# Output rows of a chunked attention: seven block products of 256 columns per pair of chunks in place of eight

## The reference, cut to what matters

```python
o = jnp.transpose(_chunk_abc(q, k, v, s), (0, 2, 1, 3))      # 16 heads, 64 slots, values of 128
g = (hidden_states @ Wg).reshape(b, t, H, DV)
o = o * jax.lax.rsqrt(jnp.mean(jnp.square(o), axis=-1, keepdims=True) + EPS) * g_norm_weight
o = o * (g * jax.nn.sigmoid(g))
return o.reshape(b, t, VALUE_DIM) @ Wo                        # VALUE_DIM = 2048, Wo is 2048 x 512
...
x = _layernorm(x + _L0_attn_ref(x, ...), axis=-1)
```

## Time and profile before

| | |
|---|---|
| median of 3 runs | 1337.37 us (1337.26 to 1337.68) |
| the profiled execution, its own time | 1337.4 us |
| its span, first to last instruction | 1335.7 us |
| TensorE busy | 1326.4 us, 99% |
| VectorE busy | 813.2 us, 61% |
| ScalarE busy | 473.0 us, 35% |
| GpSimd busy | 276.4 us, 21% |
| mean granted TensorE clock | 0.999 |

### The profile page before, as it was taken

The page is one execution under the profiler, slowest core; times in us unless marked ns, Lnnn a source line. Parts: engine busy times, 40 slices in busy tenths (PEclk is TensorE's granted clock), DMA queues, the critical chain, the costliest instruction groups (busy, mean ns, idle before and its releaser), DMA issues.

```text
span 1335.7 us, 20339 instructions
## 1 busy us (share of the span) xinstructions
PE 1326.4 (99%) x8160; PEld 1143.3 (86%) x8160; DVE 813.2 (61%) x1559; ACT 473.0 (35%) x1391; POOL 276.4 (21%) x254
## 2 busy tenths in 40 slices
PE   9999999999999999999999999999999999999998
PEld 7888888888888888888888888888888888888886
DVE  5665666556666565656655566666556667656754
ACT  5333333343333433333234333343333333432221
POOL 3012311132112301231113111231023113122211
PEclk9999999999999999999999999999999999999999
DMA  6000200010000100010001000010000210000010
GB/s 205 17 1 0 56 1 16 1 32 25 16 1 25 32 17 1 9 48 5 12 0 48 10 17 1 25 32 17 1 22 27 64 33 0 1 0 32 18 46 32
DMA packets 35357, 31.73 MB, mean 24 GB/s; under 512 B 7617, under 2 KB 28097, under 8 KB 35265
## 3 DMA queue, kind: packets, MB, share of 16 engines
q1 hardware_dynamic: 35264, 30.44, 7.6%
HBM read 26.24 MB, written 4.19 MB: 23 GB/s over the span
## 4 chain that ended last, share of the span: by engine, by line
PE 97%; DVE 1%; DMA 0%; ACT 0%; issue 0%; POOLq 0%; SPq 0%; POOL 0%
PE p L899 20%; PE p L901 19%; PE p L900 19%; PE t L948 5%; PE s L973 3%; PE o L1090 3%; PE xb L1045 2%; PE o L1026 2%; PE o L1024 2%; PE t L1090 2%; PE p L973 2%; PE s L1379 2%; PE s L1381 2%; PE s L1380 2%; PE xb L998 2%; PE o L1023 2%
## 5 line engine op out<-in xcount | busy, mean ns | idle before, releaser
L899 PE MATMUL p<-wvg_hi,xt_hi 128*128 128x512 f32 x512 | 206.0, 402 | 0.1
L900 PE MATMUL p<-wvg_lo,xt_hi 128*128 128x512 f32 x512 | 199.8, 390 | 0.0
L901 PE MATMUL p<-wvg_hi,xt_lo 128*128 128x512 f32 x512 | 199.8, 390 | 0.0
L542 ACT ACTIVATE v_tok<-p 128x256 f32<-128x256 f32 x128 | 49.8, 389 | 318.8 <-PE p L901 318.8
L708 DVE SCALAR_TENSOR_TENSOR gate<-th,p 128x256 f32<-128x256 f32 x128 | 54.0, 422 | 164.4 <-ACT th L546 160.9
L899 PE MATMUL p<-xt_hi,wsqk_hi 128*128 128x512 f32 x380 | 148.4, 391 | 0.0
L900 PE MATMUL p<-xt_lo,wsqk_hi 128*128 128x512 f32 x380 | 148.2, 390 | 0.0
L901 PE MATMUL p<-xt_hi,wsqk_lo 128*128 128x512 f32 x380 | 147.8, 389 | 0.0
L491 POOL TENSOR_TENSOR orstd<-ovar,minus_half 128x8 f32<-128x8 f32 x32 | 52.4, 1639 | 447.1 <-DVE ovar L843 447.1
L482 POOL TENSOR_TENSOR v_lo<-v_tok,v_hi 128x256 fp32r<-128x256 f32 x96 | 83.8, 886 | 198.9 <-ACT v_hi L551 198.9
L901 PEld LDWEIGHTS p<-wvg_hi,xt_lo 128*128 128x128 f32 x512 | 96.1, 188 | 21.3
(11 more groups left out here) (241 smaller groups left out, 2844.0 us busy)
## 6 DMA issues: line engine op xcount, KB each, us to landing
raw<-in_L_attn_Wv SPq DMA_DIRECT2D x32, 128.0 KB, 2.4
raw<-in_L_attn_Wg SPq DMA_DIRECT2D x32, 128.0 KB, 2.9
raw<-in_L_attn_Wo SPq DMA_DIRECT2D x16, 256.0 KB, 2.8
out<-acc SPq DMA_DIRECT2D x16, 256.0 KB, 2.1
acc<-in_L_attn_hidden_states SPq DMA_DIRECT2D x3, 1024.0 KB, 7.5
raw<-in_L_attn_Ws SPq DMA_DIRECT2D x8, 256.0 KB, 2.8
raw<-in_L_attn_Wq SPq DMA_DIRECT2D x8, 256.0 KB, 2.8
raw<-in_L_attn_Wk SPq DMA_DIRECT2D x8, 256.0 KB, 3.3
```

The lines of the kernel that those rows point to most:

```text
L542: nc.scalar.activation(v_tok[:, c, :], PB[bk][:, 0:VW], ACT.Copy).then_inc(v_done, 1)
L899: nc.tensor.matmul(out_, lh, rh, start=(k == 0), stop=False)
L900: nc.tensor.matmul(out_, lh, rl, start=False, stop=False)
L901: last = nc.tensor.matmul(out_, ll, rh, start=False, stop=(k == n - 1))
```

## The change

The rows of two chunks a and b by the two heads are seen as a 2x2 matrix of blocks (A11 = chunk a, head 0; A12 = chunk a, head 1; A22 = chunk b, head 1; A21 = chunk b, head 0), and the weights as a 2x2 matrix of blocks of 128x256. Their product is formed from seven block products in place of eight (Winograd's form). Three of them use blocks of y (M1, and M2 with M4 in one bank), four use sums S1 to S4 of blocks of y; the weights get sums T1 to T4. A product is still three matmuls, now of 256 columns: 42 in a cell. The 2x2 of sums of results is formed by accumulating in PSUM (U2 onto M1's bank, C onto M5's bank, the last product onto U2's) and by VectorE, which adds each bank to `acc` at each of these states: eight additions of 256 columns and four of 512.

- VectorE: `y_sums`, four sums of 128x128 per half, the first half's ahead of `keep_keys(1)`; `y_low` of 384 columns.
- ScalarE: `y_high` copies A21 apart (128 columns) and the high part of three blocks; `sums_high`, the high part of S1 to S4; `rows_scaled`, `rows_high` for the weights.
- GpSimd: `sums_low` twice at the beginning of its part of a cell; `row_sums`, `row_lows` for the weights once per pair of heads.
- TensorE: new waits, for `s_lo_done` before M5, and before a bank is accumulated onto for VectorE's reading of it (`m1_read`, `m5_read`, `u2_read`).
- Buffers move, `wo` has seven blocks, TensorE's turn of pz waits for `c_read`, its weights products for `added`; in the last cell the turns of V wait for `added`.

```diff
-P_USES = ["vg0", "vg1", "wo0", "wo1", "wo2", "wo3", "vg2", "vg3", "s", "q", "k", "a0", "a1"]
+P_USES = ["vg0", "vg1", "wo0", "wo1", "vg2", "vg3", "s", "q", "k", "a0", "a1"]
...
+        def row_sums(pool, J):
+            w1, w2 = row_pieces
+            t = sums[:].rearrange("p h a t -> p (h a t)").rearrange("p (k n) -> p k n", k=4)
+            pool.wait_ge(wo_scaled, 2 * (J + 1))
+            nc.gpsimd.tensor_tensor(t[:, 0, :], w1[:, HALF:D], w1[:, 0:HALF], ALU.subtract).then_inc(wo_summed, 1)
...
+        def sums_low(pool, prev, i):
+            pool.wait_ge(s_hi_done, prev.count(2, i + 1))
+            nc.gpsimd.tensor_tensor(s_lo[i][:], sums[:, i, :, :], s_hi[i][:].bitcast(F32),
+                                    ALU.subtract).then_inc(s_lo_done, 1)
+
+        def cell_gpsimd(pool, cell, J=None, wo_J=None, last=False):
+            if not first(cell):
+                sums_low(pool, cell.shifted(-1), 0)
+                sums_low(pool, cell.shifted(-1), 1)
...
+            nc.scalar.activation(a21[:, half, :], Y_BANK[half][:, 3 * P:], ACT.Copy).then_inc(a21_done, 1)
+            nc.scalar.activation(yt_hi[:, half, :, :].rearrange("p a t -> p (a t)"), Y_BANK[half][:, 0:3 * P],
                                  ACT.Copy).then_inc(yt_hi_done, 1)
+
+        def sums_high(act, cell, half):
+            act.wait_ge(s_summed, cell.shifted(-1).count(8, 4 * half + 4))
+            nc.scalar.activation(s_hi[half][:], sums[:, half, :, :], ACT.Copy).then_inc(s_hi_done, 1)
...
             if not first(cell):
                 act.wait_ge(ok_summed, cell.count(1, 1))
                 slots_high(act)
                 values_high(act, cell, 0)
+                sums_high(act, cell, 1)
...
+        def y_sums(dve, cell, half):
+            prev = cell.shifted(-1)
+            blk = Y_BANK[half][:].rearrange("p (a t) -> p a t", a=CH)
+            out_ = sums[:, half, :, :]
+            dve.wait_ge(yt_hi_done, prev.count(2, half + 1))
+            nc.vector.tensor_tensor(out_[:, S1, :], a21[:, half, :], blk[:, A22, :], ALU.add).then_inc(s_summed, 1)
+            nc.vector.tensor_tensor(out_[:, S3, :], blk[:, A11, :], a21[:, half, :], ALU.subtract).then_inc(s_summed, 1)
+            dve.wait_ge(s_summed, prev.count(8, 4 * half + 1))
+            nc.vector.tensor_tensor(out_[:, S2, :], out_[:, S1, :], blk[:, A11, :], ALU.subtract).then_inc(s_summed, 1)
+            dve.wait_ge(s_summed, prev.count(8, 4 * half + 3))
+            nc.vector.tensor_tensor(out_[:, S4, :], blk[:, A12, :], out_[:, S2, :], ALU.subtract).then_inc(s_summed, 1)
...
             gate_vector(dve, cell, 0)
             keep_keys(0)
             gate_vector(dve, cell, 1)
+            if not first(cell):
+                y_sums(dve, cell, 0)
             keep_keys(1)
             keep_keys(2)
             if not first(cell):
                 y_low(dve, cell, 0)
+                y_sums(dve, cell, 1)
                 y_low(dve, cell, 1)
...
             if not first(cell):
-                add_rows(dve, cell, 1)
+                add_m1(dve, cell, 1)
+                add_m24(dve, cell, 1)
+                add_m5(dve, cell, 0)
+                add_m5(dve, cell, 1)
+                add_u2(dve, cell, 0)
+                add_u2(dve, cell, 1)
...
+            for i in range(2):
+                bk, before = p_turn(cell, f"wo{i}")
+                wait_read(pe, p_read, before)
+                pe.wait_ge(yt_lo_done, prev.count(2, i + 1))
+                row_product(SB[i][:, 0:HALF], parts[i], A11, B11, True, m1_done)
+                row_product(PB[bk][:, 0:HALF], parts[i], A12, B21, True, None)
+                row_product(PB[bk][:, HALF:D], parts[i], A22, T4, True, m24_done)
+            for i in range(2):
+                pe.wait_ge(s_lo_done, prev.count(2, i + 1))
+                row_product(C_BANK[i][:, 0:HALF], mixed[i], S1, T1, True, m5_done)
+            for i in range(2):
+                pe.wait_ge(m1_read, prev.count(2, i + 1))
+                row_product(SB[i][:, 0:HALF], mixed[i], S2, T2, False, u2_done)
+            for i in range(2):
+                pe.wait_ge(m5_read, prev.count(2, i + 1))
+                row_product(C_BANK[i][:, 0:HALF], mixed[i], S4, B22, False, c_done)
+            for i in range(2):
+                pe.wait_ge(u2_read, prev.count(2, i + 1))
+                row_product(SB[i][:, 0:HALF], mixed[i], S3, T3, False, a_done)
...
             if last:
+                pe.wait_ge(added, cell.count(2, 0))
                 car.prep_turn(pe, 0, PREP[0])
```

More of the change, by code:

```diff
@@ L604, in cell_scalar @@
             values_high(act, cell, 2)
+            if wo_J is not None and wo_J > 0:
+                rows_scaled(act, wo_J)
             act.wait_ge(pz_turned, cell.count(1, 1))
@@ L621, in cell_scalar @@
                 keys_scalar(act, nxt)
-            if wo_J is not None:
-                for i in (7, 8):
-                    split_high(act, wo_J, i, (rows, wo_J * (B * CH)))
             if last:
@@ L755, in cell_vector @@
+        def cell_vector(dve, cell, last=False):
             nxt = cell.shifted(1)
@@ L953, in turned_y @@
             pe.wait_ge(y_done, cell.count(2 * CH, 0))
-            turned(Y_BANK[half], [y[:, c, h, :] for c in (2 * half, 2 * half + 1) for h in range(2)], y_turned)
-        def output_rows(pe, cell, c):
-            prev = cell.shifted(-1)
-            bk, before = p_turn(cell, f"wo{c}")
-            wait_read(pe, p_read, before)
-            pe.wait_ge(yt_lo_done, prev.count(2, c // 2 + 1))
-            if c == 0:
-                if prev.batch == 0:
-                    pe.wait_ge(wo_lo_done, (prev.b // B) * 2 + 2)
-            split_product(PB[bk][:], [((yt_hi[:, c // 2, c % 2, h, :], yt_lo[:, c // 2, c % 2, h, :]),
-                                       (wo_hi[:, h, :], wo_lo[:, h, :])) for h in range(2)], rows)
+            a, b = 2 * half, 2 * half + 1
@@ new lines, in turned_y, with row_product @@
+            turned(Y_BANK[half], [y[:, a, 0, :], y[:, a, 1, :], y[:, b, 1, :], y[:, b, 0, :]], y_turned)
+        def row_product(out_, left, which, right, begin, done):
+            hi, lo = left
+            nc.tensor.matmul(out_, hi[:, which, :], wo_hi[:, right, :], start=begin, stop=True, skip_group_check=True)
+            nc.tensor.matmul(out_, hi[:, which, :], wo_lo[:, right, :], start=False, stop=True, skip_group_check=True)
+            mm = nc.tensor.matmul(out_, lo[:, which, :], wo_hi[:, right, :], start=False, stop=True, skip_group_check=True)
+            if done is not None:
+                mm.then_inc(done, 1)
@@ new lines, in output_rows @@
+        def output_rows(pe, cell):
+            prev = cell.shifted(-1)
+            if prev.batch == 0:
+                pe.wait_ge(wo_lo_done, (prev.b // B) * 4 + 4)
+            parts = [(yt_hi[:, i, :, :], yt_lo[:, i, :, :]) for i in range(2)]
+            mixed = [(s_hi[i], s_lo[i]) for i in range(2)]
+            for i in range(2):
[14 more added lines that the diff above has]
+                row_product(C_BANK[i][:, 0:HALF], mixed[i], S4, B22, False, c_done)
+            for i in range(2):
+                pe.wait_ge(u2_read, prev.count(2, i + 1))
+                row_product(SB[i][:, 0:HALF], mixed[i], S3, T3, False, a_done)
```

229 lines of the change are left out of this document (156 added, 73 removed).

## The result

The changed kernel takes **1463.86 us** (median of 4 runs, 1459.88 to 1468.61) against 1337.47: ratio 1.0946, 95% interval 1.0929 to 1.0963. That is 126.4 us more; the forecast was 99 more, and its range ended at 1455, 9 us short.

A forecast was written before the change was run, and what follows sets the result against it. TensorE, busy 99% of the span, was taken to bound the kernel. Cell stalls 84, weight-split cells 11, last cell 2.4 and tail 2 made 99 us on 1337.4: 1436 us, range 1392 to 1455.

The forecast's parts named there:

- Steps 1 to 6: One cell's queues put in order on its clock: stalls 3.25 less 0.6, +2.7 us per cell, 31 cells, +84 us.
- stall 2: TensorE's M5 of half 1 waits for GpSimd's low parts of the sums: 0.65 us.
- stall 3: TensorE's U2 of half 1 waits for VectorE's third addition, which reads the same bank: 1.1 us.
- stall 4: TensorE's product C waits for VectorE's first addition of M5, which reads the same bank: 0.7 us.
- stall 5: TensorE waits at the running values for VectorE's hv copies: 0.25 us.
- stall 1: TensorE's third running sum waits for VectorE's second product of keys (hk), behind four sums: 0.55 us.
- Step 4: VectorE's ok less top, both operands in SBUF, and GpSimd's e_tok_lo lock each other out: 0.3 us over mere sharing.
- Seven cells with weight splits: GpSimd's sums' low parts come before the next weights' splits, so v_lo is late for TensorE: +1.6 us each, +11 us.
- the clock: Rival: TensorE's pauses drop the clock to 1.2 GHz, up to 4.9 us a cell, 150 us: 1590, half 1510; 4%.
- Row weights: Their added sums, low parts and ScalarE passes in eight cells fit where GpSimd idles: zero.
- Throughput alone: Rival: TensorE loses only what VectorE cannot fit, 1.5 us per cell, +47: 1384 to 1390 us; 10%.
- The other side: Rival: TensorE's waits vanish and only the columns count, 19 us gained: 1318 us; 3%.

The follow-up runs named there:

- the spread order: Changed kernel's work reordered in cells 1 to 30: row products taken apart, standing between projections and running values, other engines' queues following; first measured 1374.06 us.
- no lock: Changed kernel with one added wait: GpSimd's e_tok_lo starts only after VectorE's ok less top is done; 1447.99 us.
- the pauses filled: Changed kernel with unneeded 128-column matmuls into an unused part of a bank where TensorE waits; 1447.74 us.
- the last run: The spread order after its mending, with VectorE's copy hv of chunk 0 moved ahead of pz; 1334.90 us.
- the weight splits first: Changed kernel with GpSimd making the next weights' three low parts ahead of the sums' low parts, in seven cells; 1444.36 us.
- the keys first: Changed kernel with VectorE doing the second and third product of keys (hk) ahead of the first half's four sums; 1479.10 us.

## Why the prediction was right and wrong

**Direction and mechanism held.** The kernel is slower because TensorE waits five times a cell for operations that stand late in VectorE's and GpSimd's queues; the runs without sums and without additions and the spread order show it.

**The gain (0.6 a cell) was too large**: 0.46, since a matmul of 256 columns takes 0.120 and not the 0.1165 that one group of three had suggested. That is 4 us over 31 cells.

**Steps 1 to 6, the cell.** On the prediction's clock (705.65 taken for 602.75) the third running sum starts at 606.05 (said 606.17), M5 of half 1 at 610.69 (610.83), U2 of half 1 at 612.54 (612.66), C at 613.67 (613.71), the running values at 615.20 (615.1): nothing is off by more than 0.15. From start to start, with 0.12 for each matmul between and 0.22 for the first behind a pause, stall 2 is 713.59 - 712.91 - 0.36 = 0.32 (said 0.65), stall 3 is 715.44 - 714.05 - 0.36 = 1.03 (1.1), stall 4 is 716.57 - 715.44 - 0.46 = 0.67 (0.7), stall 5 is 3.34 - 3.10 = 0.24 (0.25); stall 1 is 15.8 / 32 = 0.49 by the list of waits (0.55). Stall 2 was too large mainly because the products before it are slower, so TensorE asks later. The 0.15 us that I put before each start for the semaphore and the weights are 0.05 before it (hk ends at 708.90, TensorE starts at 708.95) and 0.10 behind it (713.59 to 713.81 is 0.22 in place of 0.12). I missed a sixth, small pause: M1 of half 1 starts at 711.76, 0.19 behind the matmul before, and the next follows at 711.95, which makes 0.14. The cell came to 38.85 in place of 38.7, and the smaller gain of the columns is in that: 30 x 0.15 = 4.5 us.

**Step 4, the lock.** Confirmed by the run with no lock: 681 against 1087 ns, and 0.4 us a cell. This agrees with the Trainium skill (SBUF — State Buffer, section "SBUF: two separate sides"), whose rule the prediction quotes: in the cell above ok less top is issued 0.54 us before the end of e_tok_lo and lasts 0.40 longer than alone. The run without sums adds that it is not one culprit: with e_tok_lo gone, v_lo takes its place.

**Seven cells with weight splits, +11**: 7 x (40.4 - 38.83) = 11.0 us in the run with the pauses filled, where the clock has no part. As forecast, and this wait is removed by GpSimd's order alone.

**Row weights, 0: wrong.** I looked whether GpSimd has the time, which it has, and not at whom its work locks out. These seven cells take 39.26, 0.42 more than the plain ones: 3 us. In such a cell GpSimd makes low parts of the row weights until 691.8, and VectorE's scan, with two SBUF operands, lasts 2.38 us beside them, 1.23 in the next cell (729.77):

```profile
690.50 2.38 DVE L751 TENSOR_TENSOR_SCAN rz_t<-e_t 128x512 f32<-128x512 f32 x1 [0.70 <-ACT e_t L590]
692.92 3.35 DVE L755 RECIPROCAL rz_t<-rz_t 128x512 f32<-128x512 f32 x1
696.19 1.22 DVE L768 TENSOR_TENSOR ww_t<-s,causal 128x512 f32<-128x512 f32 x2
...
689.25 2.55 POOL L505 TENSOR_TENSOR wo_lo<-sums,wo_hi 128x512 fp32r<-128x512 f32 x2
...
697.55 1.13 PE L1237 MATMUL o<-v_tok,ww_t 128*128 128x128 f32 x8 [0.39 <-DVE ww_t L768]
```

The masked weights come late, and TensorE waits 0.39 us for them. That is read from the timelines and wasn't tried alone. The other runs fit it: without the sums these cells still take 0.43 more than the plain ones (38.06 against 37.63), without the additions, where VectorE has room, nothing (36.70).

**Last cell and tail, 2.4 + 2.** From the start of the last cell to the end it is 200.4 us, before 193.1: +7.3, of which one cell's 2.7 belongs to the term above, so 4.6 against 4.4. Cell 30, which I took as plain, has 1.8 more (40.67); which wait that is was not looked into.

**What failed is the clock.** The prediction had it as a rival that excludes the forecast, at 4%, with 150 us or half of it, and argued that "the trace shows no pause of this pattern, and the clock stood through the 0.61 us at the start". But the forecast itself made that pattern: four pauses of 0.3 to 1.1 us within 8. And the 0.61 us at the start proves nothing, since there was no higher clock to lose. In the kernel before, the matmuls on both sides of that pause are 0.21 us apart for 128 columns, the spacing that the rival itself takes for the lower clock, and matmuls of 512 columns get faster only later (four last 1.74 us, then four 1.09):

```profile
7.80 0.42 PE L1107 MATMUL xb<-ident,acc 128*128 128x128 f32 x1
8.02 1.91 PE L1100 MATMUL t<-ident 128*128 128x128 f32 x8
9.58 1.74 PE L919 MATMUL p<-xt_hi,wsqk_hi 128*128 128x512 f32 x4
...
11.16 1.09 PE L922 MATMUL p<-xt_hi,wsqk_lo 128*128 128x512 f32 x4
```

The clock should have been a term beside the stalls, from zero up, in the upper bound of every case. Its price was wrong too: not 4.9 us in each cell, but 1.2 in seven plain cells (40.0 against 38.83) and 2.0 in the seven with weight splits (42.4 against 40.4). By the medians it is 1463.9 - 1447.7 = 16 us, and 99 + 16 + 4.5 + 3 + 1.8 + 0.2 = 124.5 of the 126.4 measured. The rule of the Trainium skill (TensorE: Matmul & The Clock Gate, section "A second HAM failure mode: psum-queue depth-cycling"), which I had quoted and not priced, agrees with these runs as far as this: short idles between groups of matmuls brought the clock down, and filling them kept it up. Whether changes of bank have a part was not tried.

**The rivals.** Throughput alone (1384 to 1390) was refuted for this order: the waits have causes that add, 1.17 and 2.10. But its thought, that VectorE's work fits or nearly fits, is what the spread order shows: the same work in 35.62 us. The other side, that the waits vanish, needed another order than the kernel's, and the 3% for this kernel was fair. In that order the last run reaches 1334.9 and not 1318: 30 cells gain 0.37 each, 11 us, and the last cell with the tail, which keeps the old order, takes 201.7 us where it took 193.1.

**What stays open**: why the clock falls in two of each four cells while the plain ones with the same stalls 1 to 5 keep it, and why it falls in 7 cells with the weight splits first and in only 4 with the keys first, where the pauses are longest. Stalls 1 and 2 without 3 and 4 (additions dropped), or 3 and 4 without 1 and 2 (sums dropped), took the clock down in no plain cell, so it needs them together or longer pauses; more than this the runs do not tell.

## What to carry to other kernels

Where one engine is 99% busy, a cheaper product brings only its columns, and each value that it takes or gives in the same breath must be placed as far ahead as the queues of the other engines are long: here the same work cost 126 us in one order (16 of them by the clock) and nothing in another. Put every step of the change on the clock of one cell, queue by queue; that gave the starts of the products that waited to 0.15 us before the kernel ran. Then add what the waits themselves trigger, the clock above all, as a term and not as a rival.

## What was not expected of the hardware

- Pauses of 0.3 to 1.1 us, four in 8 us, with TensorE busy in between, took the granted clock to 0.59 in the 3 us behind them; matmuls of 256 columns were then 0.21 us apart, of 512 columns 0.43, and it cost 16 us in all. Nine unneeded matmuls per cell in the pauses, fifteen in those with weight splits, kept it at 0.998, with no fall in cells 1 to 30.
- Two SBUF operands on VectorE beside GpSimd: pz 1.76 us in place of 0.68, the scan 2.38 in place of 1.23, ok less top 1.09 in place of 0.68. GpSimd is held up likewise when it comes second: e_tok_lo 1.50 in place of 1.02. In the run without sums, what GpSimd did next took the place of what had moved away.
- A matmul behind a pause delays its follower by 0.10 us (713.59 to 713.81 is 0.22, where the others are 0.12 apart).
